# Attention scores on row halves of the array, with both score passes rotating over three pairs of PSUM banks

## The reference

```python
# attention, on layernorm(x)
q, k, v = (split into heads of x @ W.T + b)
q, k = _apply_rope(q, cos, sin), _apply_rope(k, cos, sin)
scores = einsum('bhqd,bhkd->bhqk', q, k) / sqrt(dh)
scores = where(causal, scores, -inf)
out = einsum('bhqk,bhkd->bhqd', softmax(scores), v)
x = x + out @ Wo.T + bo
# mixture of experts, on layernorm(x): 8 experts, the best 2 for each token, capacity 153 a batch
einp = buf.at[expert, position].add(token)          # a scatter
o = einsum(silu((einp @ w_c_fc + b) * (einp @ w_gate + b)), w_c_proj) + b
x = x + sum of the two gathered rows, weighted by softmax of the two router logits
```

## Time and profile before

| | |
|---|---|
| the profiled execution's own time | 1391.76 us |
| its span, first to last instruction | 1389.9 us |
| runs, median (lowest to highest) | 1383.12 us (1378.21 to 1386.19) |
| mean granted TensorE clock, share of full speed | 0.943 |
| attention steps, first score matmul to the last step with new scores | 39.80 to 594.65 us |
| first expert matmul | 626.45 us |

### The profile page before, as it was taken

The page is one execution under the profiler, slowest core; times in us unless marked ns, Lnnn a source line. Parts: engine busy times, 40 slices in busy tenths (PEclk is TensorE's granted clock), DMA queues, the critical chain, the costliest instruction groups (busy, mean ns, idle before and its releaser), DMA issues.

```text
span 1389.9 us, 25801 instructions
## 1 busy us (share of the span) xinstructions
PE 1238.5 (89%) x8360; PEld 1023.6 (74%) x8360; DVE 729.6 (52%) x1512; ACT 496.3 (36%) x988; POOL 697.0 (50%) x984
## 2 busy tenths in 40 slices
PE   3699999999898989988899999999999999997830
PEld 3465656566565656548899999999999999997730
DVE  5777776858676767556333343343333433333336
ACT  2145444535353535454223332333233332332100
POOL 4334243343425251267755665576656764634445
PEclk9699999999999999999999999999999999998865
DMA  5766545444434453432312211131122112102247
GB/s 138 216 208 193 177 115 144 109 132 103 138 93 139 100 149 93 137 124 60 96 62 91 70 62 62 64 98 54 66 78 87 54 58 70 64 28 72 69 131 249
DMA packets 82333, 147.86 MB, mean 106 GB/s; under 512 B 9263, under 2 KB 59832, under 8 KB 78142
## 3 DMA queue, kind: packets, MB, share of 16 engines
q1 hardware_dynamic: 64576, 111.37, 28.1%
q0 software_dynamic: 7936, 26.60, 5.6%
q10 hardware_dynamic: 9728, 8.67, 2.0%
HBM read 93.05 MB, written 53.61 MB: 106 GB/s over the span
## 4 chain that ended last, share of the span: by engine, by line
PE 45%; another core or an unknown queue 2%; DVE 1%; POOL 1%; issue 1%; DMA 0%; DVEq 0%; ACT 0%; POOLq 0%; ACTq 0%
PE ps L77 44%; PE ps L1264 1%; DVE raw L1427 1%; POOL wg_hi L1544 1%; POOL wf_hi L1544 0%; DMA wg_hi<-slot_outputs,slot_all 0%; DVE al L1417 0%; DVEq L1454 0%; DVE ah L1408 0%; POOLq L1572 0%; ACT hid L1349 0%; ACT fc L1360 0%; DVE xl L1332 0%; DVE gated L1455 0%
## 5 line engine op out<-in xcount | busy, mean ns | idle before, releaser
L1491 POOL TENSOR_TENSOR al<-hid,ah 128x384 fp32r<-128x384 f32 (+1 forms) x176 | 187.4, 1065 | 232.9 <-DVE ah L1408 232.9
L1360 ACT ACTIVATE fc<-ps,b_fc 128x384 f32<-128x384 f32 (+1 forms) x192 | 115.5, 602 | 482.4 <-PE ps L77 441.2
L1455 DVE SCALAR_TENSOR_TENSOR gated<-ps,b_gate,fc 128x384 f32<-128x384 f32 (+1 forms) x192 | 123.4, 643 | 268.1 <-PE ps L77 220.2
L794 DVE TENSOR_REDUCE mx<-ps 128x2 f32<-128x256 f32 (+3 forms) x256 | 206.6, 818 | 67.1 <-PE ps L408 56.5
L577 ACT ACTIVATE probs<-ps 128x512 f32<-128x512 f32 (+1 forms) x256 | 125.6, 541 | 73.8 <-PE ps L434 72.0
L408 PE MATMUL ps<-kst,qst 65*128 65x256 f32 (+2 forms) x512 | 151.7, 380 | 0.0
L1442 DVE TENSOR_TENSOR o_sb<-ps,b_proj 128x256 f32<-128x256 f32 x80 | 33.9, 424 | 179.0 <-PE ps L77 175.1
L569 ACT ACTIVATE probs<-ps 128x256 f32<-128x256 f32 (+1 forms) x128 | 62.6, 490 | 164.4 <-PE ps L425 150.0
L445 PE MATMUL ps<-probs,v_sb 128*32 128x512 f32 (+3 forms) x1024 | 98.8, 459 | 14.2 <-DVE v_sb L822 14.0
L77 PE MATMUL ps<-xh,wg_hi 128*128 128x384 f32 (+1 forms) x384 | 104.4, 353 | 5.0 <-DVE gated L1455 4.2
L935 POOL TENSOR_TENSOR rope_c<-qk_b,rope_table 128x512 f32<-128x512 f32 x32 | 42.7, 1333 | 128.9 <-ACT qk_b L605 128.7
(11 more groups left out here) (181 smaller groups left out, 2577.5 us busy)
## 6 DMA issues: line engine op xcount, KB each, us to landing
qk_parts<-hilo SPq DMA_DIRECT2D x32, 512.0 KB, 3.1
qst<-qk_parts SPq DMA_DIRECT2D x64, 256.0 KB, 4.8
kst<-qk_parts SPq DMA_DIRECT2D x64, 256.0 KB, 5.2
slot_tokens<-zeros POOLq DMA_DIRECT2D x12, 816.0 KB, 5.6
rows<-slot_tokens SPq DMA_DIRECT2D x24, 384.0 KB, 3.7
slot_outputs<-o_sb SPq DMA_DIRECT2D x72, 128.0 KB
raw<-in_wf SPq DMA_DIRECT2D x8, 1024.0 KB, 6.1
raw<-in_wg SPq DMA_DIRECT2D x8, 1024.0 KB, 7.6
```

Source lines behind the costliest of these rows:

```text
L794: V.reduce_max(mx[:, g % 2, i, 2 * pr:2 * pr + 2], both[:, :, 0:P * (i + 1)], AXX)\
L1360: A(fc[:, hc % 2, 0:width], ps[:, FC + hc % 2, 0:width], ACT.Identity, bias=b_fc[:, e, hc:hc + 1]).then_inc(fc_out, 1)
L1455: V.scalar_tensor_tensor(gated[:, hc % 2, 0:width], ps[:, GATE + hc % 2, 0:width], b_gate[:, e, hc:hc + 1], fc[:, hc % 2, 0:width], ALU.ad ...
L1491: G.tensor_tensor(al[:, at, 0:width], hid[:, hc % 2, 0:width], ah[:, at, 0:width].bitcast(F32), ALU.subtract).then_inc(al_done, 1)
```

## The change

1. The stacks hold three combinations instead of four (small x small goes): 48 rows, 49 with the maximum. Two heads of a pair stand on the two halves of the partitions (rows 0 to 48 and 64 to 112), so that each score matmul takes one half of the array's rows, and the two halves write to the two banks of a pair. The mask matmul is per half too: 64 rows of `pick_bf`, each with two columns, one of them scaled by 2^-88.
2. Both passes take a bank pair from three (banks 0 to 5) in turn (`USES`, which goes 2, 0, 1, 2, 0, 1 and so on). So the scores of the first pass wait for the exponentials two slots before, and those of the second for the row maximum of the slot before (`pair_freed`). The exponentials are all over two heads at once.
3. Probabilities of a step are kept whole (`PROB_AT`), and the four blocks of the value product stand in slots 6, 7 of a step and 0, 1 of the next, in bank 6 together with `M` and `A`. The other pieces have bank 7.
4. Every part of the side work has its slot in a table, often slots ahead of the old one. The loop is written out. The sine product and the move of the values go from VectorE to GpSimd, the large part from GpSimd to ScalarE, the value bias is put into the output bias once at the start, and the values are copied by ScalarE. VectorE's `normalise` of the next input goes from slot 5 of step 0 to slot 1 of step 3 of the batch before.
5. `load_stack` takes eight DMAs, `send_max` two.

```diff
-ZROW = NP * DH
-MROW = ZROW + 1
+HALF = P // 2
+MROW = (NP - 1) * DH
 ROWS = MROW + 1
+PAIRS = GH // 2
-        ident_bf = sb("ident_bf", [P, P], BF16)
+        pick_bf = sb("pick_bf", [P, 2, P], BF16)
-        qst = sb("qst", [ROWS, NG, GH, T], F32R)
-        kst = sb("kst", [ROWS, NG, GH, T], F32R)
+        qst = sb("qst", [P, NG, PAIRS, T], F32R)
+        kst = sb("kst", [P, NG, PAIRS, T], F32R)
-        probs = sb("probs", [P, 2, GH, T])
+        probs = sb("probs", [P, 2, GH, PROB_AT[TT]])
+        PIECES = (
+            (0, "X", 0), (3, "X", 1), (5, "H", 0), (6, "Q", 0), (7, "H", 1), (9, "Q", 1), (11, "Q", 2), (13, "L", 0),
+            (14, "R", 0), (16, "Q", 3), (18, "F", 0), (19, "T", 0), (21, "T", 1), (23, "O", 0), (25, "O", 1),
+            (26, "V", 0), (29, "V", 1),
+        )
+        PV_AT = (6, 7, 8, 9)
+        COS_SIN_AT = (5, 12, 14, 19)
+        SMALL_AT = (11, 19, 21, 37)
+        STORE_QK_AT = (16, 17, 20, 37)
+        LOAD_STACK_AT = (3, 13, 23, 29)
+        NORM1_AT = (25,)
+        X1_AT = (25, 26)
...
+        def pair_freed(b, g, u, which):
+            k = 2 * (32 * b + 8 * g + u) + which
+            pair = USES[k % len(USES)]
+            for back in range(k - 1, -1, -1):
+                at, w = back // 2, back % 2
+                if USES[back % len(USES)] == pair and use_there(at, w):
+                    return (red_done, at + 1) if w == 0 else (exp_done, at - 16 + 1)
...
+            def first(b, g, u):
+                for hh, half in enumerate(rows_of):
+                    mm(pair[:, hh, bass.ts(i, P)], pick_bf[half, 0], causal_bf[half],
+                       start=True, stop=False, skip_group_check=True)
+                width = max(2 * P, P * (i + 1))
+                for hh in range(2):
+                    rows = slice(HALF * hh, HALF * hh + MROW)
+                    last = mm(pair[:, hh, 0:width], qst[rows, g, pr, bass.ts(i, P)], kst[rows, g, pr, 0:width],
+                              start=False, stop=True, skip_group_check=True)
+                last.then_inc(p1_done, 1)
...
-                V.tensor_copy(v_sb[:, :, :, 0:DH],
-                                  v_next[:].rearrange("p t (h r) -> p t h r", h=HEADS)).then_inc(v_moved, 1)
+                        G.tensor_copy(v_sb[:, :, :, 0:DH], v_next[:].rearrange("p t (h r) -> p t h r", h=HEADS))\
+                            .then_inc(v_moved, 1)
+                    ins = G.tensor_tensor(rope_s[:, n % 2, :], qk_b[:, n % 2, :], sin, ALU.mult)
```

More of the change, by code:

```diff
@@ L275, in last_piece @@
[L275 to L289, removed]
-            return None
@@ new lines, in in_batch, with bank_of @@
+        def in_batch(kind, b):
+            first, last = {"X": (-1, 6), "Q": (-1, 6), "V": (-1, 6), "T": (1, 8), "O": (1, 8), "H": (2, 9), "L": (2, 9),
+                           "R": (2, 9), "F": (2, 9)}[kind]
+            return first <= b <= last
+        FIRST = [(kind, n) for at, kind, n in PIECES if kind in "XQV"]
+        def bank_of(b, kind, n):
+            if b == -1:
+                return ps[:, FIRST.index((kind, n)), :]
+            return ps[:, LOW if kind in "MPA" else HIGH, :]
@@ L304, in before_late @@
         def before_late(b):
-            return [(g, u) for g in range(NG) for u in range(SLOTS)
-                    if not (isinstance(b, int) and b == BATCH) or (g, u) < LATE_FROM]
+            return [(g, u) for g in range(NG) for u in range(SLOTS) if b < BATCH or (g, u) < LATE_FROM]
         @block.sync
@@ L340, in body_slot, with send_max @@
+            def send_max(t):
+                wait(sp, negmax_out, t + 1)
+                wait(sp, p2_done, TILES2 * (t - 3))
+                for hh in range(2):
+                    row = HALF * hh + MROW
+                    sp.dma_start(qst[row:row + 1, t % 4].bitcast(F32), negmax[hh:GH:2, t % 2, :].bitcast(F32))\
+                        .then_inc(ld_max, 16)
             def body_slot(b, g, u):
-                if isinstance(b, int) and (b, g, u) in FIRST_LOAD_AT:
+                if (b, g, u) in FIRST_LOAD_AT:
@@ L362, in body @@
+                for t in step_due(SEND_MAX_AT, b, g, u, 1):
+                    send_max(t)
+                for n, i in due(LOAD_STACK_AT, b, g, u):
+                    if n < 3 and there(i, 1, 7):
+                        load_stack(i, n + 1)
+                    if n == 3 and there(i, 0, 6):
+                        load_stack(i + 1, 0)
             def body(b):
@@ new lines, in body, with late @@
+                    high_bank(b, g, u)
+            def late(b, g, u):
+                low_bank(b, g, u)
+                high_bank(b, g, u)
+            pe.wait_ge(ld_const, 16)
+            for kind, n in FIRST:
+                if kind != "X":
+                    pe.wait_ge(w_split, {("Q", 0): 1, ("Q", 1): 2, ("Q", 2): 1, ("Q", 3): 2}.get((kind, n), 3))
+                high_piece(kind, -1, n, None)
+            pe.wait_ge(ld_w, 16 * 11)
+            pe.wait_ge(bv_ready, 1)
+            for c in range(CK):
+                last = mm(bank_of(-1, "X", 1)[:, 0:C], bv_wide[:, c, :], wo[:, c, :], start=(c == 0), stop=(c == CK - 1))
@@ L547, in _ @@
+            last.then_inc(bo_done, 1)
             pe.wait_ge(made, 5)
             pe.wait_ge(ld_ones, 32)
-            body(0)
-            body(1)
-            with pe.Fori(2, 7) as b:
+            pe.wait_ge(v_out, 2)
+            pe.wait_ge(bo_out, 1)
+            for b in range(BATCH + 1):
                 body(b)
-            body(7)
-            body(8)
-            rt["late_slot"]["pe"] = piece
+            rt["late_slot"]["pe"] = late
         @block.scalar
@@ L783, in body_slot @@
-                if (g, u) == (1, 6) and there(b, 2, 9):
-                    slots(chain, b, 0)
-                if (g, u) in ((0, 6), (1, 1), (1, 2)) and there(b, 2, 9):
-                    route(chain, b, ((0, 6), (1, 1), (1, 2)).index((g, u)))
-                if there(b, 0, 7):
+                for part, i in due(ROUTE_AT, b, g, u):
+                    if there(i, 2, 9):
+                        route(i, part)
+                for part, i in due(PLACE_AT, b, g, u):
+                    if there(i, 2, 9):
+                        slots(i, part)
@@ L788, in body_slot @@
+                for n, i in due(PROB_OUT_AT, b, g, u):
+                    if there(i, 2, 9):
+                        probabilities(i)
+                if b < BATCH:
                     wait(dve, p1_done, 8 * s + u + 1)
@@ L1619 @@
         "consts": constants(),
-        "rows": np.stack([np.zeros(NG * GH * T, np.float32), np.ones(NG * GH * T, np.float32)]),
+        "ones": np.ones((1, NG * PAIRS * T), np.float32),
     }
```

859 lines of the change are left out of this document (432 added, 427 removed), and 7 rows, old and new, of the table PIECES.

## The result

The changed kernel takes 1536.07 us (median of 4 runs, 1534.66 to 1543.13) against 1384.65 us before, a ratio of 1.1095, 95% interval 1.1015 to 1.1174. The forecast was 1307 us with a range up to 1352, so it is wrong in sign.

A forecast was written before the change was run, and what follows sets the result against it. TensorE was taken to bound the kernel. A loop batch changes by -13.2 + 4 - 1.3 = -10.5 us; six give -63, batch 7 -10, batch 0 -4 and +3, the end -2: together -76, so 1307 us, range 1262 to 1352.

The forecast's parts named there:

- Scores on halves: Attention's score passes: the two row halves run side by side, 18.4 us a batch instead of 31.6, so -13.2.
- weights in turn: Rival on score passes: weights load one after the other, 24.3 us a batch, 1348 us in all; chance 0.15.
- not side by side: Rival on score passes: the halves don't run at once, 36.8 us a batch, 1438 us in all; chance 0.05.
- More changes of shape: TensorE in a loop batch: 24 new trips between matmul shapes cost +4 us, bounds 0 and 11.
- Idle time and clock: TensorE's waits and slow clock in a loop batch: 7.7 us instead of 9.0, so -1.3; bounds 2 and 18.
- the fourth: Rival: waits at slots 17, 24 to 26 and 32 slow TensorE's clock, 20 us a batch, about 1395 us; chance 0.05.
- Other engines: Per loop batch, VectorE falls to some 46.5 us and GpSimd rises to some 33; no cost while TensorE bounds.

The follow-up runs named there:

- e12: e11 with the third batch's x rows loaded at the start behind the second group's stack, not behind all four: 1349.87 us, 0.9702 of the kernel before.
- e8: The changed kernel with its two-part stack loads each cut into one load per part, 12 a group instead of 8, same places: 1414.82 us, 1.0064.
- e10: The kernel before with its stack loads' source running first over the two parts, same number, rows and bytes: 1632.44 us, 1.1592.
- e9: e8 with all four stack loads issued early and the residual's x rows loaded at slot 28 of the batch before: 1399.49 us, 0.9956.
- e11: e9 with the second part of the router's choice on VectorE moved from slot 17 to slot 16: 1364.41 us, 0.9795.
- e5: The changed kernel with all four stack loads issued early and the residual's x rows loaded at slot 28 of the batch before: 1478.08 us, 1.0499.
- e4: The kernel before with its four stack loads issued in slot 7 of the step before instead of slot 0: 1458.28 us, 1.0444.

## Why the prediction was wrong, step by step

*Scores on halves: right.* The changed kernel's passes in the dense stream, which answer to the earlier trace rows:

```profile
303.25 0.23 PE L437 MATMUL ps<-causal_bf,pick_bf 64*128 64x128 bf16 x2
...
303.49 0.23 PE L455 MATMUL ps<-later_bf,pick_bf 64*128 64x128 bf16 x2
...
303.79 0.23 PE L437 MATMUL ps<-causal_bf,pick_bf 64*128 64x128 bf16 x2
...
307.35 0.23 PE L437 MATMUL ps<-causal_bf,pick_bf 64*128 64x128 bf16 x2
307.39 0.48 PE L442 MATMUL ps<-kst,qst 48*128 48x512 f32 x2
307.80 1.07 PE L483 MATMUL ps<-probs,v_sb 128*32 128x512 f32 x8
```

Both heads at 256 columns take 0.24 us and at 384 they take 0.30, where I had put 0.25 and 0.30. The halves run side by side, and the rivals "weights in turn" (0.38 in all shapes) and "not side by side" are out.

*More changes of shape: right within its bounds.* The pass of 512 columns ahead of a value block takes 0.45 us, 0.1 over the 0.35 of a half's stream. Ahead of another pass it takes 0.36, in e12:

```profile
306.85 0.23 PE L457 MATMUL ps<-later_bf,pick_bf 64*128 64x128 bf16 x2
...
307.21 0.23 PE L439 MATMUL ps<-causal_bf,pick_bf 64*128 64x128 bf16 x2
```

Together: the work fell from 481.1 to 405.8 us in e12 (393.6 in the changed kernel; windows of 3 us blur the split between work and clock loss where the clock changes within one), 75.3 / 7.75 = 9.7 us a batch, against 13.2 - 4 = 9.2 forecast; the two terms are not measured apart. e12's 65.1 us a batch stand beside a forecast of 63.4.

*Idle time and clock: this step failed.* I put 7.7 us a batch where the changed kernel has (140.2 + 121.3) / 7.75 = 33.7. Idle time alone is 16.6 us a batch, past the 10 us at which I called myself wrong. The places I named were nearly right, slots 0, 17 and 24. What I got wrong is in one clause: "17 DMAs of about 0.6 us", and for the start "four more stack DMAs of 0.6 us". I priced a load by its issue on an empty queue and assumed that its transfer lands as before. Cutting the source dimension by pairs and halves had put the parts outermost. e8 and e10 show that this order sets how long the loads take, and the DMA shares of 0.13 and 0.97 that it sets how many DMA engines serve them. It was in the change's code: the source was `d c (h t)`, and is `h c d p t`. The Trainium skill's rule told above would have priced it, and I did not weigh it against the change. The start, forecast at +3 us, came out at +42.

*The rival that came true is the fourth*, waits that slow the clock: condition "from 18 us", place and sign as written, size not, since it counted one wait of 2 us in each step and 1395 us. It had 5%.

*Other engines: "cost nothing while TensorE bounds" failed at one place.* The busy times are near the forecast: VectorE 50.3 us a batch (48.6 in e12) for 46.5, GpSimd 32.1 for 33. But I had seen `over` take 1.78 us for 8 elements and named GpSimd's work as a likely cause, then priced it at nothing. With the rotation's sine product and the values' move on GpSimd, the router's chain at slot 17 is held for 3.4 us in e9 (1.26 + 0.97 + 0.94 + 0.97 less 4 x 0.19), TensorE waits 4.25, and e11 measured it at 22 to 35 us in the whole. The changed kernel has these waits too, of up to 4.3 us. One of the router's operations over the whole run, before and changed, by its mean of 184 and 731 ns:

```profile
L720 DVE SCALAR_TENSOR_TENSOR logits<-onehot,logits 128x32 f32<-128x32 f32 x8 | 1.5, 184 | 0.1
L763 DVE SCALAR_TENSOR_TENSOR logits<-onehot,logits 128x32 f32<-128x32 f32 x8 | 5.8, 731 | 0.1
```

*The sum.* The attention's work -87, idle +105, clock +98, start +42, end -15: +143, the difference of the two spans. Of the distance between the changed kernel and e12, 186 us, the order of the source is 121, places 15, the router 35 and the start's load 15; in points of the ratio 10.3, 1.1, 1.6 and 0.9 of 13.9, which is the fairer split of the router's part. What stays open: why e12's start is still 11 us later than before's, beside the 32 more loads on SP (48 for 16); and whether places and transfers split in the same way in another order of undoing, since e5's edits were worth 58 us (6 points) while the loads were slow and 15 (1.1) after.

## What to carry to other kernels

When a change re-cuts a DMA's source, compare the outermost dimension on both sides before and after, not only bytes and issues: here 2 instead of 16 cost 121 us, more than the 75 us of TensorE's work that the change saves. In these traces an issue on SP's queue that took much over its usual 0.6 us stood behind transfers that did not drain; look there before moving places. And put chains of small VectorE operations where GpSimd is idle; one number in a table was worth 1.6%.

## What the runs showed that I had not expected

- Loads whose source is outermost 2 long move 54 GB/s at a DMA share of 0.13, and SP is held for up to 10.7 us by one issue.
- VectorE operations on 32 columns take 0.19 us alone and up to 0.94 to 1.26 beside a GpSimd operation, ending with it; reductions of the same size in the same chain (0.19) are not held.
- The clock can come back late though the stream is dense. I had taken the halves for a cause, but e4, with the full-height matmuls of before, shows 15 us of it at 0.50 with TensorE busy throughout, behind 3.1 us idle:

```profile
336.00:341.00 5.00, 1.92 (x18) 1.03 (x18) 3.51 (x6) 0.77 (x2) 1.39 (x7) 0.81 0.79 194
341.00:356.00 15.00, 15.00 (x67) 9.62 (x66) 4.94 (x15) 6.72 (x12) 2.81 (x14) 0.50 0.33 71
356.00:359.00 3.00, 3.00 (x37) 1.68 (x36) 2.12 (x4) 1.40 (x3) 0.00 (x0) 0.98 0.00 0
```

The forecast had 2.9 us for such a stretch, from the earlier trace rows. At half clock 15 us are 7.5 lost, more than the wait.
